# Products with values moved from the middle of a pass's transposes to its head (cross-attention and a mixture of experts, one core)

## The chip, the cores and the metric

One core of a Trainium2 chip runs the whole kernel. The metric is the device time in microseconds (us). Before the change it is 366.25 us, the median of three runs (363.2 to 366.45 us).

## The reference

Eight samples (B = 8) of 112 rows (S) and width 256 attend, with 16 heads of width 16, to a context of 375 rows per sample; then comes a mixture of 32 experts. The attention is what the change touches:

```python
qh = _split_heads(layernorm(x)); kh = vh = _split_heads(ctx)
scores  = einsum('bhqd,bhkd->bhqk', qh, kh) + mask
weights = softmax(scores)
att     = einsum('bhqk,bhkd->bhqd', weights, vh)      # heads joined again
x = x + relu(att @ wo_w.T + wo_b)
x = x + experts(layernorm(x))      # gate, 4 of 32 experts, and a shared one
```

The experts' stage reads the attention's result for all samples, and starts when the attention's block has ended.

## The kernel before, in words

The kernel is written for the engines directly: each engine has its own program, in the order in which it issues, and counting semaphores tie them together. There is no scheduler.

**Tiling of the attention.** Four heads (HPQ = 4) form a group; a sample has four groups (QPB = 4), so there are NQ = 32 groups. TensorE runs a loop over passes p = 0 to 33 (L414). In pass p it works on three groups at once:

- `score(p)` (L358): the scores of group p, four products of 32 rows by 112 by 375, one for each head, into four PSUM banks.
- `turn_prob(4(p-1)+j)` for j = 0 to 3 (L335): the shifted scores `z` of group p-1 are transposed, three pieces of 112 by 125 for a head. The heads' shift by their maximum was done meanwhile: VectorE takes the mask and the maximum of every head (L555), then GpSimd lowers heads 0 and 1 (L289), VectorE head 2 (L565) and ScalarE head 3 (L496). Each head's transposes wait for its own one of these.
- `value(p-2)` (L371): the products of group p-2's weights `pT` with the values, twelve products of 125 rows by 32 by 112, into one bank (SUM_BANK) that holds the sample's sums. It waits until the fourth exponential of group p-2 is there (L373) and, for a sample's first group, for `values_ok` and `sums_ok`.

**The ring of two banks.** Everything that TensorE transposes for ScalarE in this stage goes through two PSUM banks in turn (T_BANK, T_BANK + 1). A unit n, a head's transposes for example, may be written only when ScalarE has read unit n-2 (`bank_of`, L304 to L309). ScalarE reads a head with one exponential, `weigh` (L479), from PSUM to `pT`. `ring_units` (L52) lists the units in order: four heads in each pass and then, at the end of most passes, one more unit by `close(p)` (L349): half the keys of the next sample (k0, k1, three transposes, L316), its queries (q, two transposes, L324) or the attention of an earlier sample (ctxT, two transposes, L332). Passes 3, 28, 29, 30 and 32 have no closing unit.

**Other work in a pass.** In each fourth pass from 8 on, `project` (L397) multiplies with the output weights, after the scores; in passes 6, 10, 14 and so on `turn_sums` (L387) transposes a sample's sums. ScalarE copies these sums out in passes 5, 9 and so on, after the pass's second exponential (`copy_sums`, L475), when all four groups of values have arrived.

**Around it.** Sync issues the loads of context and mask two samples ahead, and behind the masks the loads of the experts' weights (L240 to L250). The last loads of this stage are waited for in the next stage only.

The order inside a pass that the change is about is that of TensorE's loop:

```python
for j in range(HPQ):
    if 0 <= p - 1 < NQ:
        turn_prob(HPQ * (p - 1) + j)
    if j == 1 and p >= 2:
        value(p - 2)
close(p)
```

Of the kernel before, what the change touches and what calls it, by code (L numbers as in the profile page):

```python
# [22 lines left out]
def xattn_moe_kernel(nc, x, ctx, mask, wo_w, wo_b, gw, gb, w1, b1, w3, b3, w2, b2,  # L23
# [61 lines left out]
    with ExitStack() as st:  # L85
# [81 lines left out]
        def attention(block, sba):  # L167
# [129 lines left out]
            def _(pe):  # L297
                def warm(n, bank=SUM_BANK):

                    for _ in range(n):  # L300
                        nc.tensor.matmul(ps[:, bank, :].rearrange("p (r c) -> p r c", c=P), ident[:],  # L301
                                         ident[:].unsqueeze(1).to_broadcast([P, BANK // P, P]), start=True, stop=True)
# [32 lines left out]
                def turn_prob(n):  # L335
                    bank = bank_of(("prob", n))
                    p, j = n // HPQ, n % HPQ
                    if j in POOL_HEADS:
                        pe.wait_ge(by_pool, len(POOL_HEADS) * p + POOL_HEADS.index(j) + 1)
                    elif j in DVE_HEADS:  # L340
                        pe.wait_ge(by_dve, len(DVE_HEADS) * p + DVE_HEADS.index(j) + 1)
                    else:
                        pe.wait_ge(by_act, len(ACT_HEADS) * p + ACT_HEADS.index(j) + 1)
                    for c in range(KT):
                        ins = nc.tensor.transpose(bank[0:KP, c * S:(c + 1) * S], z[:, n % RING, c * KP:(c + 1) * KP],  # L345
                                                  ident[0:S, 0:S])
                    ins.then_inc(ring_full, 1)

                def close(p):  # L349
                    for kind, b in closing(p):  # L350
                        if kind == "q":
                            turn_queries(b)
                        elif kind == "ctxT":
                            turn_att(b)
                        else:
                            turn_keys(b, int(kind[1]))

                def score(p):  # L358
                    b, g = p // QPB, p % QPB
                    if g == 0:  # L360
                        pe.wait_ge(ring_read, max(UNIT["q", b], UNIT["k0", b]) + 1)
                    if g == 2:
                        pe.wait_ge(ring_read, UNIT["k1", b] + 1)
                    if p:
                        pe.wait_ge(masked, HPQ * p)
                    for j in range(HPQ):
                        rows = slice(32 * j, 32 * j + 32)
                        nc.tensor.matmul(ps[0:S, S_BANK + j, 0:SK], qT[rows, b % 2, g // 2, g % 2, :],  # L368
                                         kT[rows, b % 2, g // 2, :], start=True, stop=True).then_inc(scores, 1)

                def value(p):  # L371
                    b, g = p // QPB, p % QPB
                    pe.wait_ge(ring_read, UNIT["prob", HPQ * p + HPQ - 1] + 1)  # L373
                    if g == 0:
                        pe.wait_ge(values_ok, b + 1)
                        if b:
                            pe.wait_ge(sums_ok, b)
                    for c in range(KT):
                        for j in range(HPQ):
                            h = 8 * (g // 2) + 2 * j + g % 2  # L380
                            ins = nc.tensor.matmul(ps[32 * j:32 * j + VC, SUM_BANK, g * S:(g + 1) * S],  # L381
                                                   vaug[:, b % 2, c, h, :],
                                                   pT[:, (HPQ * p + j) % RING, c * S:(c + 1) * S],
                                                   start=(c == 0), stop=(c == KT - 1))
                    ins.then_inc(valued, 1)

                def turn_sums(b):  # L387
                    pe.wait_ge(sums_ok, b + 1)
                    if b:
                        pe.wait_ge(prj_ok, b)  # L390
                    else:
                        pe.wait_ge(wo_copied, 1)
                    for g in range(QPB):
                        ins = nc.tensor.transpose(ps[0:S, AUX_BANK, g * P:(g + 1) * P], sums[:, g * S:(g + 1) * S], ident[:])
                    ins.then_inc(turned, 1)

                def project(b):  # L397

                    pe.wait_ge(ring_read, UNIT["ctxT", b] + 1)
                    pe.wait_ge(att_ok, 2 * b + 2)  # L400
                    for k in range(DK):
                        ins = nc.tensor.matmul(ps[0:S, AUX_BANK, 0:D], attT[:, k, :], woT[:, k, :],
                                               start=(k == 0), stop=(k == DK - 1))
                    ins.then_inc(projected, 1)
# [7 lines left out]
                turn_keys(0, 1)  # L412
                warm(1)
                for p in range(NQ + 2):  # L414
                    if p < NQ:
                        score(p)
                    if p < 2:
                        warm(2)
                    if p == 0:
                        pe.wait_ge(bias_in, 16 * 4)  # L420
                        nc.tensor.transpose(ps[:, AUX_BANK, 0:NE], b1r[:], ident[0:NE, 0:NE])
                        nc.tensor.transpose(ps[:, AUX_BANK, P:P + NE], b3r[:], ident[0:NE, 0:NE]).then_inc(bias_T, 1)
                    if p == 1:
                        pe.wait_ge(bias_copied, 2)
                        pe.wait_ge(wo_in, 16)
                        for t in range(DK):
                            for k in range(DK):
                                ins = nc.tensor.transpose(ps[:, AUX_BANK, (k * DK + t) * P:(k * DK + t + 1) * P],
                                                          wo_raw[:, t, k * P:(k + 1) * P], ident[:])
                        ins.then_inc(bias_T, 1)  # L430
                    if p % QPB == 0 and p >= 2 * QPB:
                        project(p // QPB - 2)
                    if p % QPB == 2 and p > QPB:
                        turn_sums(p // QPB - 1)
                    for j in range(HPQ):
                        if 0 <= p - 1 < NQ:
                            turn_prob(HPQ * (p - 1) + j)
                        if j == 1 and p >= 2:
                            value(p - 2)
                    close(p)  # L440

                pe.wait_ge(masked, HPQ * NQ)
# [712 lines left out]
```

## Time and profile before

| | before |
|---|---|
| median of 3 runs (us) | 366.25 (363.2 to 366.45) |
| profiled execution: its own time / its span (us) | 361.01 / 359.2 |
| TensorE matmul busy, share of the span | 290.2 us, 81% |
| VectorE busy | 222.8 us, 62% |
| GpSimd busy | 181.7 us, 51% |
| ScalarE busy | 150.9 us, 42% |
| mean granted TensorE clock | 0.914 |

All times in the rows further down are microseconds from the start of the span of this one profiled execution, whose own time is 5.24 us below the median of the three runs. The passes 0 to 33 of the attention take from about 13 us to about 150 us; the experts' stage follows from 160 us. A matmul's row is its own duration, and matmuls overlap, so the distance between the starts of two rows tells more than their durations. One product or transpose in float32 shows as one or two rows of the trace, so that "x6" at L345 is the transposes of two heads, "x24" at L381 one `value`, and "x8" at L368 one `score`.

### The profile page before, as it was taken

What the parts mean: (1) busy time and instruction counts of PE and PEld (TensorE: products, weight loads), DVE (VectorE), ACT (ScalarE), POOL (GpSimd) and SP (SyncE); (2) the same over time, 40 slices, a digit from 0 to 9 for tenths busy, and PEclk for the clock granted to TensorE, in tenths of its full rate; (3) what the DMA queues carried; (4) which work ended last, traced back from release to release, by engine and by line L of the source; (5) the groups of instructions that cost most, each with busy time, mean ns of one, the idle gap of its engine ahead of it and who ended that gap; (6) DMA issues with size and microseconds to landing.
All of it is one profiled execution on the core that took longest, in us unless ns stands there. A gap on an engine that the chain in (4) does not pass through costs nothing.

```text
span 359.2 us, 7134 instructions
## 1 busy us (share of the span) xinstructions
PE 290.2 (81%) x2301; PEld 202.9 (56%) x2301; DVE 222.8 (62%) x708; ACT 150.9 (42%) x403; POOL 181.7 (51%) x188
## 2 busy tenths in 40 slices
PE   8999999999999999899898022199999999999000
PEld 3466666666666667656474011077778777776000
DVE  1678877767777778276969200065666666656097
ACT  1267666666566666515110000044545545544000
POOL 7266757565657566110027777307556555556200
PEclk9999999999999999999999555589999999999655
DMA  6795888959794900009502333385555455542495
GB/s 150 206 78 149 261 240 244 265 172 292 218 326 138 308 5 2 2 13 295 162 0 79 109 110 114 116 101 161 162 167 157 148 167 158 155 154 76 159 242 168
DMA packets 54013, 55.92 MB, mean 156 GB/s; under 512 B 18925, under 2 KB 45562, under 8 KB 53466
## 3 DMA queue, kind: packets, MB, share of 16 engines
q1 hardware_dynamic: 49610, 43.94, 45.6%
q0 software_dynamic: 4368, 11.52, 9.8%
q8 instruction: 21, 0.34, 0.4%
q14 instruction: 14, 0.11, 0.1%
HBM read 35.03 MB, written 20.41 MB: 154 GB/s over the span
## 4 chain that ended last, share of the span: by engine, by line
PE 29%; DVE 9%; POOL 9%; issue 4%; DMA 3%; ACT 0%; POOLq 0%; DVEq 0%; SPq 0%
PE ps L878 14%; POOL expert_rows L794 9%; PE ps L893 7%; DVE x L1119 4%; PE ps L870 3%; PE ps L887 2%; DMA b<-expert_out 1%; PE ps L816 1%; DMA expert_rows<-normed,slots 1%; DMA expert_out<-hs,to 1%; DMA xg<-expert_rows 1%; POOL expert_out L799 1%; PE ps L846 1%; PE ps L808 0%; PE ps L841 0%
## 5 line engine op out<-in xcount | busy, mean ns | idle before, releaser
L289 POOL TENSOR_SCALAR z<-z,zmax 112x375 f32<-112x375 f32 x64 | 78.7, 1241 | 52.7 <-DVE zmax L555 52.7
L799 POOL DMA_INDIRECT expert_out<-hs,to x59 | 56.6, 959 | 50.3 <-DVE hs L1088 35.2
L555 DVE CUSTOM_DVE_ANT_0 z<-ps,mask_sb 112x375 f32<-112x375 f32 x128 | 62.5, 546 | 28.8 <-PE ps L368 28.8
L483 ACT ACTIVATE pT<-ps 125x336 f32<-125x336 f32 x128 | 50.7, 448 | 38.1 <-PE ps L345 37.7
L878 PE MATMUL ps<-w,xgT 128*128 x236 | 64.1, 396 | 0.0
L345 PE MATMUL ps<-ident,z 112*125 112x112 f32 x384 | 56.6, 283 | 0.2 <-ACT pT L483 0.2
L345 PEld LDWEIGHTS ps<-ident,z 112*125 112x125 f32 x384 | 47.3, 188 | 15.4 <-ACT pT L483 7.3
L1106 DVE TENSOR_TENSOR hb<-ps,b 128x256 f32<-128x256 f32 x59 | 25.1, 425 | 49.1 <-PE ps L878 49.1
L794 POOL DMA_INDIRECT expert_rows<-normed,slots x32 | 32.4, 1014 | 35.1 <-DVE normed L1059 25.7
L878 PEld LDWEIGHTS ps<-w,xgT 128*128 128x128 f32 x236 | 43.5, 196 | 10.0 <-issue 1.8
L870 PE MATMUL ps<-ident,xg 128*128 128x128 f32 x118 | 24.0, 287 | 30.2 <-DMA xg<-expert_rows 30.2
L935 ACT COPY xgT<-ps 128x256 f32<-128x256 f32 x59 | 22.0, 373 | 46.4 <-PE ps L870 46.4
L893 PE MATMUL ps<-w2s,hs 128*128 x118 | 36.0, 387 | 0.0
L942 ACT COPY hs<-ps 128x128 f32<-128x128 f32 x59 | 15.7, 266 | 47.8 <-PE ps L887 47.8
L870 PEld LDWEIGHTS ps<-ident,xg 128*128 128x128 f32 x118 | 14.8, 146 | 33.2 <-DMA xg<-expert_rows 25.9
L1112 DVE TENSOR_TENSOR hh<-hb,sg 128x128 f32<-128x128 f32 x59 | 17.3, 293 | 19.5 <-ACT sg L947 17.0
L368 PE MATMUL ps<-kT,qT 32*112 32x375 f32 x256 | 28.8, 519 | 0.0
L381 PE MATMUL ps<-pT,vaug 125*32 125x112 f32 x768 | 25.0, 263 | 0.6 <-ACT pT L483 0.6
L1088 DVE COPY hs<-ps 128x256 f32<-128x256 f32 x59 | 24.5, 415 | 1.1 <-PE ps L893 0.6
L301 PE MATMUL ps<-ident 128*128 128x512 f32 x44 | 23.6, 669 | 1.6 <-POOL ident L256 1.6
L565 DVE TENSOR_SCALAR z<-z,zmax 112x375 f32<-112x375 f32 x32 | 23.7, 741 | 0.0
L1119 DVE SCALAR_TENSOR_TENSOR x<-b,gate,x 112x256 f32<-112x256 f32 x32 | 14.9, 484 | 8.9 <-DMA b<-expert_out 8.1
(159 smaller groups left out, 348.8 us busy)
## 6 DMA issues: line engine op xcount, KB each, us to landing
xg<-expert_rows SPq DMA_DIRECT2D x59, 128.0 KB, 2.3
expert_rows<-zero SPq DMA_DIRECT2D x14, 512.0 KB, 10.0
w2s<-in_L_ffn_w SPq DMA_DIRECT2D x2, 2048.0 KB, 9.6
b<-in_L_ffn_b SPq DMA_DIRECT2D x2, 2048.0 KB, 14.1
b<-expert_out SPq DMA_DIRECT2D x8, 448.0 KB, 9.3
ctx_sb<-in_ctx SPq DMA_DIRECT2D x8, 375.0 KB
mask_sb<-in_mask_Bx1xSxS_ff SPq DMA_DIRECT2D x8, 164.1 KB, 2.4
expert_out<-hs,to POOLq DMA_INDIRECT x59, 2.8
```

The source lines that it names most:

```text
L289: pool.tensor_scalar(z[:, n % RING, :], z[:, n % RING, :], zmax[:, n % RING:n % RING + 1], None, ALU.subtract).then_inc(by_pool, 1)
L345: ins = nc.tensor.transpose(bank[0:KP, c * S:(c + 1) * S], z[:, n % RING, c * KP:(c + 1) * KP], ident[0:S, 0:S])
L368: nc.tensor.matmul(ps[0:S, S_BANK + j, 0:SK], qT[rows, b % 2, g // 2, g % 2, :], kT[rows, b % 2, g // 2, :], start=True, stop=True).then_i ...
L483: nc.scalar.activation(pT[:, n % RING, :], ps[0:KP, T_BANK + at % 2, 0:KT * S], ACT.Exp).then_inc(ring_read, 1)
L555: nc.vector.tensor_tensor_reduce(out=z[:, n % RING, :], in0=ps[0:S, S_BANK + j, 0:SK], in1=mask_sb[:, b % 2, :], scale=-1.0 if j in ACT_HE ...
L794: pool.indirect_dma_start(xs, bass.IndirectOffsetOnAxis(ap=slots[:, b, r:r + 1], axis=0), normed[:, b, :], None).then_inc(scattered[r], 16)
L799: pool.indirect_dma_start(ys, bass.IndirectOffsetOnAxis(ap=to[:, j:j + 1], axis=0), y_sb[:, j % 4, :], None).then_inc(y_sent[j % 4], 16)
L870: ins = nc.tensor.transpose(ps[:, T_BANKS[j % 2], k * P:(k + 1) * P], xg[:, j % 4, k * P:(k + 1) * P], ident[:])
L878: ins = nc.tensor.matmul(ps[:, U_BANKS[j % 2], 0:2 * INTER], xgT[:, j % 4, k, :], w13[:, k, bass.ds(owner_of(words, j), 1), :].rearrange(" ...
L893: nc.tensor.matmul(ps[:, Y_BANKS[j % 2], 0:D], hT[:, j % 4, :], w2s[:, bass.ds(owner_of(words, j), 1), :].rearrange("p o c -> p (o c)"), s ...
L1106: TT(hb[:, j % 2, :], ps[:, U_BANKS[j % 2], 0:2 * INTER], b13[:, bass.ds(owner_of(words, j), 1), :].rearrange("p o c -> p (o c)"), ALU.add ...
L1119: ins = nc.vector.scalar_tensor_tensor(x2[:, b, :], rows[:, TOPK * b + r, :], gate[:, b, r:r + 1], x2[:, b, :], ALU.mult, ALU.add)
```

## The change

`value(p - 2)` is issued at the head of pass p, ahead of `score(p)`, where before it stood between the transposes of the pass's second and third head. Nothing else is changed: the same instructions with the same waits and the same semaphores, in another order on TensorE alone. No DMA is moved, and no other engine's program.

```diff
@@ -412,6 +412,8 @@
                 turn_keys(0, 1)
                 warm(1)
                 for p in range(NQ + 2):
+                    if p >= 2:
+                        value(p - 2)
                     if p < NQ:
                         score(p)
                     if p < 2:
@@ -435,8 +437,6 @@
                     for j in range(HPQ):
                         if 0 <= p - 1 < NQ:
                             turn_prob(HPQ * (p - 1) + j)
-                        if j == 1 and p >= 2:
-                            value(p - 2)
                     close(p)
 
                 pe.wait_ge(masked, HPQ * NQ)
```

## Rows read from the trace of the kernel before

**Rows 1.** The page: busy tenths of 40 equal slices, and the granted clock
```profile
PE   8999999999999999899898022199999999999000
PEclk9999999999999999999999555589999999999655
```

**Rows 2.** Windows by stage: busy us (instructions) of each engine, PEclk, DMA share, GB/s
```profile
60.00:100.00 40.00, 38.08 (x469) 27.01 (x470) 29.79 (x102) 25.53 (x61) 25.23 (x22) 1.00 0.79 232
140.00:152.00 12.00, 10.80 (x142) 7.52 (x134) 5.79 (x20) 7.26 (x16) 4.11 (x4) 1.00 0.01 1
198.00:236.00 38.00, 9.24 (x27) 6.42 (x28) 3.73 (x11) 2.87 (x10) 23.33 (x25) 0.51 0.43 110
```

**Rows 3.** Timeline of TensorE, pass 17 and the start of 18: start, us, what, idle before
```profile
84.61 0.90 PE L368 MATMUL ps<-kT,qT 32*112 32x375 f32 x8
85.44 0.91 PE L345 MATMUL ps<-ident,z 112*125 112x112 f32 x6
86.28 0.78 PE L381 MATMUL ps<-pT,vaug 125*32 125x112 f32 x24
86.99 0.91 PE L345 MATMUL ps<-ident,z 112*125 112x112 f32 x6
88.11 0.54 PE L316 MATMUL ps<-ident,ctx_sb 125*128 125x125 f32 x3 [0.21 <-ACT pT L483]
88.58 0.90 PE L368 MATMUL ps<-kT,qT 32*112 32x375 f32 x8
```

**Rows 4.** Timeline of ScalarE in the same pass
```profile
86.05 0.79 ACT L483 ACTIVATE pT<-ps 125x336 f32<-125x336 f32 x2 [0.36 <-PE ps L345]
87.12 0.53 ACT L477 COPY sums<-ps 128x448 f32<-128x448 f32 x1 [0.28 <-PE ps L381]
87.60 0.79 ACT L483 ACTIVATE pT<-ps 125x336 f32<-125x336 f32 x2
```

**Rows 5.** The line of the exponential: durations min/median/max in ns, 20 to 150 us
```profile
L483 ACT ACTIVATE pT<-ps x128: 444/451/452, 20.9 to 149.0; 125x336 f32<-125x336 f32 x128
```

**Rows 6.** Timeline of pass 1, which has no value products: TensorE (weight loads PEld) and ScalarE
```profile
19.96 0.60 PE L428 MATMUL ps<-ident,wo_raw 128*128 128x128 f32 x4
20.29 0.73 PEld L345 LDWEIGHTS ps<-ident,z 112*125 112x125 f32 x6
20.40 0.81 PE L345 MATMUL ps<-ident,z 112*125 112x112 f32 x6
20.92 0.79 ACT L483 ACTIVATE pT<-ps 125x336 f32<-125x336 f32 x2 [1.22 <-PE ps L345]
21.42 0.92 PE L345 MATMUL ps<-ident,z 112*125 112x112 f32 x6 [0.21 <-ACT pT L483]
22.54 0.54 PE L316 MATMUL ps<-ident,ctx_sb 125*128 125x125 f32 x3 [0.20 <-ACT pT L483]
```

**Rows 7.** Timeline of TensorE where a pass (29) has no closing unit
```profile
136.81 0.91 PE L345 MATMUL ps<-ident,z 112*125 112x112 f32 x6
137.65 0.58 PE L368 MATMUL ps<-kT,qT 32*112 32x375 f32 x4
```

**Rows 8.** Timeline of TensorE, end of pass 31, passes 32 and 33
```profile
144.75 0.41 PE L332 MATMUL ps<-ident,att 112*128 112x112 f32 x2 [0.21 <-ACT pT L483]
145.60 1.12 PE L402 MATMUL ps<-woT,attT 128*112 128x256 f32 x4 [0.43 <-ACT attT L472]
147.29 0.78 PE L381 MATMUL ps<-pT,vaug 125*32 125x112 f32 x24
148.00 0.91 PE L345 MATMUL ps<-ident,z 112*125 112x112 f32 x6
149.46 0.78 PE L381 MATMUL ps<-pT,vaug 125*32 125x112 f32 x24 [0.55 <-ACT pT L483]
```

**Rows 9.** Timeline of TensorE where the closing unit is a pair of transposes (passes 14, 15)
```profile
75.61 0.41 PE L324 MATMUL ps<-ident,normed 112*128 112x112 f32 x2 [0.21 <-ACT pT L483]
75.95 0.90 PE L368 MATMUL ps<-kT,qT 32*112 32x375 f32 x8
```

**Rows 10.** Timeline of GpSimd in pass 17
```profile
86.29 2.44 POOL L289 TENSOR_SCALAR z<-z,zmax 112x375 f32<-112x375 f32 x2 [2.38 <-DVE zmax L555]
```

**Rows 11.** Chain of waits, start and us: the same four matmuls at either clock
```profile
233.11 1.78 PE ps L878 x4
236.09 0.86 PE ps L878 x4
```

## The prediction

> **What bounds the kernel now.** I read the slices first. TensorE is busy in eight or nine tenths from the start to about 160 us, and in this whole stretch its granted clock stays at the full level (2.4 GHz) [rows 1]. The windows say who could bind there: from 60 to 100 us TensorE has 38.1 of 40 us, VectorE 29.8, ScalarE 25.5, GpSimd 25.2 [rows 2]. A busy TensorE may still be waiting, so the timeline of a pass comes next. Pass 17 runs from 84.61 to 88.58, that is 3.97 us: scores 0.83, two heads' transposes 0.84, values 0.71, two heads' transposes and what follows 1.12, keys 0.47 [rows 3]. The reader is to see that no part waits except the closing unit (0.21 us by the profile, "<-ACT pT"). So the stage goes at the pace at which TensorE issues plus one wait a pass for a bank of the ring, and what is added between two starts on TensorE is added to the end: the experts' stage begins behind it and nothing overlaps the two.
>
> **How long a bank of the ring is held.** Call T0 to T3 the four heads' transposes, V the values, C the closing unit, S the scores. T2 starts at 86.99 [rows 3] and ScalarE's exponential on it at 87.60 [rows 4], 0.61 us later; it takes 0.45 us [rows 5], so the bank is read at 88.05, and C, which needs this bank, starts at 88.11 [rows 3]: 1.12 us from the start of a head's transposes to the next use of its bank. The transposes of two heads take 0.84 us (85.44 to 86.28), so whoever follows two heads directly waits 1.12 - 0.84 = 0.28 us. The profile counts 0.21 us of it, because the last matmul's modelled end is later than its issue.
>
> **What the change does to T2.** Today V stands between T1 and T2. T0 starts at 85.44, its exponential at 86.05 [rows 4], its bank is free at about 86.56; T1 is done at 86.28 and V covers until 86.99. With V gone T2 is ready at 86.28 and waits until 86.56: 0.28 us. T2 starts 1.12 after T0, T3 needs no wait (T1's exponential follows 0.35 us behind T0's, and T3 0.42 behind T2), and C comes 1.12 after T2 as before. So T0 to C is 2.24 us plus V elsewhere, against 2.67 with V inside: 2.24 + 0.71 - 2.67 = +0.28 us a pass.
>
> The trace of before has one pass in just the new form: pass 1, where there is no V yet. The profile shows both waits there, 0.21 us at 21.42 and 0.20 us at 22.54 [rows 6]. From the first weight load of T0 (20.29) to C (22.54) it is 2.25 us. This is the row on which I rest the term.
>
> **What V costs at its new place.** Before a C of three transposes V would start at T2 + 1.12 + 0.47 = T2 + 1.59; it needs T3's exponential, which pass 33 shows: T2 at 148.00, V at 149.46, that is T2 + 1.46 [rows 8]. Behind a C of two transposes C takes 0.34 us (75.61 to 75.95) [rows 9], so V is at T2 + 1.46 too, just on time. So V does not wait where a pass closes with a unit. S comes behind V then; that pair no row shows. The nearest rows are V then T2 (0.71 us from start to start) and C then S (0.47 for three transposes) [rows 3]. Unbroken transposes come every 0.11 us (four at L428, 19.96 to 20.40) [rows 6], so six are 0.66 and the 0.84 of rows 3 hold 0.18 for two changes of form, about 0.09 each. I take V then S at 0.71, as V then T2; the ends are 0.62 (no price for the change of form) and 0.80 (twice). Over 30 passes that is -2.7 or +2.7 us.
>
> Where a pass has no closing unit nothing covers T3's exponential. Today S follows 0.84 us after T2 (136.81 to 137.65) [rows 7]; V can start only at T2 + 1.46, so +0.62 us for each of the passes 3, 28, 29 and 30 (the profile's own figure for this wait in pass 33 is 0.55 [rows 8]).
>
> ScalarE's copy of the sums stands between the second and third exponential in seven passes. Today it runs in V's shadow (87.12, the next exponential at 87.60) [rows 4]. Now T0's exponential is at 86.05, T1's at 86.40, the copy at 86.75, and T2's exponential can begin at 87.23 instead of 86.56 + 0.61 = 87.17: +0.06, seven times, +0.4 us.
>
> The end gives something back. C of pass 31 starts at 144.75, and the projection waits for ScalarE's copy until 145.60, 0.85 us [rows 8]. V fits in there: the projection then starts at 144.75 + 0.34 + 0.71 = 145.80, and V is gone from between T1 and T2. That is 0.71 - 0.20 = 0.51 saved and 0.28 lost at T2: -0.23 us.
>
> **What is hidden.** S comes later in no chain that binds: GpSimd, the last to deliver, starts 1.68 us after S and ends at 88.73 [rows 10], and its second head is wanted by T1 of the next pass, at 88.58 + 0.83 + 0.42 = 89.83 at the earliest. That is 1.1 us of slack, and the distance from S to T0 and T1 of the next pass grows by the longer pass. Without that cover each us of lateness would be a us a pass. T2 and T3 stand 0.43 us earlier against it, but VectorE and ScalarE deliver them. No queue of Sync or GpSimd is passed by V; the loads behind the masks come up to 9 us later, and DMA is idle at 1% from 140 to 152 us [rows 2].
>
> **Sum.** 30 passes (2 to 31) x 0.28 = 8.4; 4 x 0.62 = 2.5; copies 0.4; pass 32 -0.2. Together +11.0 us. Against the profiled execution: 361.0 + 11.0 = 372.0 us. The runs' median is 5.2 us above that execution; on it the sum gives **377.3 us**, 3.0% more. Lower bound of the terms: 30 x 0.20 + 4 x 0.55 - 0.2 - 2.7 = +5.3; upper: 11.0 + 2.7 = +13.7.
>
> **Rivals.**
> 1. *Not slower: the change of form is saved and the wait doesn't come.* V no longer breaks the transposes, so a pass has three changes of form instead of four: 30 x 0.09 = 2.7 us less, and 0.5 less in pass 32: -3.2, 363.0 us. It decides if T0's exponential is read 0.84 us after T0's start rather than 1.12. For it speaks the 0.09 worked out above; against it the wait in pass 1 [rows 6], which swallows the saving, as it would here. Chance 0.06. The Trainium skill (TensorEngine Tiling (Array Packing), Key Properties) says that changing the tiling mode drains TensorE; taken alone, that rule gives this rival's time. The trace agrees that such a change costs something, and shows that the wait stands ahead of it.
> 2. *The wait only moves.* T2 waits 0.28 and C no longer does. Only the four bare passes and the copies are left, +2.7 us: 369 us. It needs T2's exponential to be sooner than T0's; pass 1 shows both waits in one pass [rows 6]. Chance 0.06.
> 3. *V waits behind the closing unit too.* The margin is 0.13 us behind keys and nothing behind a pair. If T3's exponential comes 0.2 us later than I have it in 26 passes, 5.2 us more: 382.5 us. Against it: pass 33 shows the distance directly. Chance 0.10.
> 4. *The granted clock falls.* With two short waits in a pass TensorE might be granted the lower level (1.2 GHz), at which four matmuls take 1.78 us instead of 0.86 [rows 11]. A pass at that level would take some 3.5 us more; ten of them 35 us, 412 us in all. Against it: pass 1 has both waits, and the clock falls only at 198 us, where TensorE is busy for 9 of 38 us [rows 1, 2]. Chance 0.02. The Trainium skill (TensorE: Matmul & The Clock Gate, A second HAM failure mode: psum-queue depth-cycling) says that short idles between groups of matmuls that cycle through PSUM banks can make the clock swing; no row here shows it, although one such wait a pass is there already.
>
> **Numbers.** The forecast has 0.76. About 1% (3.7 us) is what a measurement of this kernel can tell from no change. Slower by more holds the forecast and rivals 3 and 4: 0.88. Rival 2 (+0.7%) and half of rival 1 (-0.9%) are within 1%: 0.09; the other half faster: 0.03. Range: the lower bound gives 371.6, less 1.6 for runs that spread over 3.3 us: 370; the top takes in rival 3: 383. Outside are rivals 1, 2 and 4, 0.14, and a little of the forecast's own scatter.
>
> **What would show it.** Pass 17 of after: 4.3 us from S to S; in every pass a wait of about 0.2 us at L345 in front of the third head as well as at the closing unit; V starting 0.34 or 0.47 us after C, without a wait; L381 waiting about 0.5 us in passes 4, 29, 30, 31 and 33; S 0.71 us behind V; the attention's last projection some 11 us later, and the experts' stage of the same length. I am wrong if L345 shows no such wait, if V waits in most passes, or if the experts' stage changes its length.

## Result and profile after

The changed kernel takes 376.02 us (median of four runs, 374.64 to 377.63) against 365.0 us before in the same comparison: ratio 1.0306, 95% interval 1.0227 to 1.0385. It is slower, by 11 us. The forecast was 377.3 us.

I measure the attention from the start of the scores of pass 1 to the start of the values of pass 33, and call that the stage. Before it goes from 17.31 to 149.46, 132.15 us; after, from 17.06 to 159.98, 142.92 us. That is +10.77 us. The slices of the changed kernel, which answer to [rows 1]:

```profile
PE   8998898999999998899989121296999999999100
PEclk9999999999999999999999755579899999999655
```

The reader is to see that the granted clock stays full through the whole attention, so the time was not lost by a lower clock. TensorE's timeline of pass 17 shows where it was lost, the counterpart of [rows 3] (start, us, what, idle before):

```profile
89.23 0.78 PE L381 MATMUL ps<-pT,vaug 125*32 125x112 f32 x24
89.94 0.90 PE L368 MATMUL ps<-kT,qT 32*112 32x375 f32 x8
90.78 0.91 PE L345 MATMUL ps<-ident,z 112*125 112x112 f32 x6
91.89 0.92 PE L345 MATMUL ps<-ident,z 112*125 112x112 f32 x6 [0.21 <-ACT pT L483]
93.02 0.54 PE L316 MATMUL ps<-ident,ctx_sb 125*128 125x125 f32 x3 [0.20 <-ACT pT L483]
93.48 0.78 PE L381 MATMUL ps<-pT,vaug 125*32 125x112 f32 x24
94.20 0.90 PE L368 MATMUL ps<-kT,qT 32*112 32x375 f32 x8
```

The pass takes 4.26 us (89.94 to 94.20) instead of 3.97. There are two waits for a bank now, 1.12 us from the first head (90.78) to the third (91.89), and again from there to the keys (93.02). Keys to values is 0.46 us without a wait, values to scores 0.72. The list of TensorE's waits from 23 to 162 us (us in total, times, longest) begins with these entries:

```profile
PE ps L345 <- ACT pT L483: 6.6, 31, 0.2
PE ps L381 <- ACT pT L483: 2.7, 5, 0.5
PE ps L316 <- ACT pT L483: 2.4, 12, 0.2
```

L345 and L381 are what is new: before, L345 has no wait from 23 us on and L381 one, of 0.55 us in pass 33 [rows 8], while L316 had its twelve waits already (2.6 us in total). L345, the heads' transposes, waits once in each of passes 2 to 32; L381, the values, five times: in passes 4, 29, 30, 31 and 33. Nothing waits for VectorE or GpSimd. The first of the four at the end of the stage comes behind pass 28, which has no closing unit and answers to [rows 7]; the values at 143.08 are the head of pass 29:

```profile
140.60 0.81 PE L345 MATMUL ps<-ident,z 112*125 112x112 f32 x6
141.62 0.92 PE L345 MATMUL ps<-ident,z 112*125 112x112 f32 x6 [0.21 <-ACT pT L483]
143.08 0.78 PE L381 MATMUL ps<-pT,vaug 125*32 125x112 f32 x24 [0.54 <-ACT pT L483]
143.79 0.90 PE L368 MATMUL ps<-kT,qT 32*112 32x375 f32 x8
```

From the third head to the values it is 1.46 us; before, the scores followed after 0.84. And the end, the counterpart of [rows 8]:

```profile
155.50 0.41 PE L332 MATMUL ps<-ident,att 112*128 112x112 f32 x2 [0.20 <-ACT pT L483]
155.84 0.78 PE L381 MATMUL ps<-pT,vaug 125*32 125x112 f32 x24
156.55 1.12 PE L402 MATMUL ps<-woT,attT 128*112 128x256 f32 x4
159.98 0.78 PE L381 MATMUL ps<-pT,vaug 125*32 125x112 f32 x24 [0.54 <-ACT pT L483]
```

The values stand where TensorE waited for ScalarE's copy; from the closing unit to the last values it is 4.48 us (155.50 to 159.98) instead of 4.71 (144.75 to 149.46).

### The profile page after: what moved, and what is told of

Its sections match the earlier page's. It is cut to its first block, busy times and chain, and to the rows that moved or that the text cites. A ratio compares the mean times of both kernels' runs of the same rounds, so it can differ in the third digit from the quotient of the medians.

```text
span 375.6 us, 7134 instructions
## 1 busy us (share of the span) xinstructions
PE 295.6 (79%) x2301; PEld 205.4 (55%) x2301; DVE 223.0 (59%) x708; ACT 149.9 (40%) x403; POOL 182.1 (48%) x188
## 4 chain that ended last, share of the span: by engine, by line
PE 25%; issue 18%; DVE 5%; DMA 2%; SPq 2%; another core or an unknown queue 1%; ACT 1%; POOL 1%; POOLq 0%; DVEq 0%
PE ps L878 13%; PE ps L893 6%; DVE x L1119 4%; PE ps L870 3%; PE ps L887 2%; SPq L750 1%; DMA b<-expert_out 1%; DMA expert_out<-hs,to 1%; POOL expert_out L799 1%; DMA xg<-expert_rows 0%; POOLq L1127 0%; ACT sg L947 0%; ACT xgT L935 0%; SPq L755 0%
## 5 line engine op out<-in xcount | busy, mean ns | idle before, releaser
L878 PE MATMUL ps<-w,xgT 128*128 x236 | 66.0, 405 | 0.0
L345 PE MATMUL ps<-ident,z 112*125 112x112 f32 x384 | 57.0, 284 | 6.8 <-ACT pT L483 6.8
L345 PEld LDWEIGHTS ps<-ident,z 112*125 112x125 f32 x384 | 47.7, 187 | 22.2 <-ACT pT L483 12.5
L878 PEld LDWEIGHTS ps<-w,xgT 128*128 128x128 f32 x236 | 44.7, 201 | 10.6 <-issue 2.2
L381 PE MATMUL ps<-pT,vaug 125*32 125x112 f32 x768 | 25.0, 263 | 2.7 <-ACT pT L483 2.7
L301 PE MATMUL ps<-ident 128*128 128x512 f32 x44 | 23.3, 660 | 1.6 <-POOL ident L256 1.6
L381 PEld LDWEIGHTS ps<-pT,vaug 125*32 125x32 f32 x768 | 17.3, 109 | 7.7 <-ACT pT L483 5.7
```

What stands on the lines that cost most here:

```text
L878: ins = nc.tensor.matmul(ps[:, U_BANKS[j % 2], 0:2 * INTER], xgT[:, j % 4, k, :], w13[:, k, bass.ds(owner_of(words, j), 1), :].rearrange(" ...
```

## Experiments

Of each I give the stage as defined above, from one profile. In four of the twelve profiles (the changed kernel's third, values behind the third head, and the last two kernels below) the granted clock fell to about half for 3.4 us from 18 us on, and pass 1 is some 1.7 us longer; there I compare from the scores of pass 2, where the kernel before has 126.45 us. These are the four in which TensorE had waited longest in pass 0 for the load of `b3r`, one of the experts' biases: 1.46 to 1.89 us, against 0.52 to 1.33 us in the eight others.

**The changed kernel and the one before again.** Both unchanged.

> The changed kernel again, for the experts' stage, which was 5.6 us longer in its profile than in that of before. If that belongs to the change, it is there again; if it was ScalarE's 3.2 us pause and the lower clock behind it in that one execution, this profile has the attention at 142.9 us again and an experts' stage within 2 us of that of before.

> The kernel before once more, for a second profile. Stage from the scores of pass 1 to the values of pass 33: 132.2 us. The pause of ScalarE near the tenth block of the experts (about 3 us, seen in both profiles of the changed kernel and not in the one of before): if it belongs to the change it is absent here; if it comes with the chip or the moment, it can be here too.

> The changed kernel a third time beside it: stage 142.9 us. If the pause belongs to the change it is here and not in the kernel before; if not, the two profiles agree on it or it falls either way.

Stage of the changed kernel: 142.90 us in the first repetition (its median 376.94 us), and 144.62 in the second with the low clock in pass 1 (136.51 from the scores of pass 2, the same to 0.01 us as in the first profile). Before: 132.15 again. The first repetition, in four runs, was at 1.0336 (1.0273 to 1.04) of the one before. The attention's length is thus repeatable to 0.02 us, and the +10.8 us are the change's.

The experts' stage is another matter. From its first transposes to the end of the span the profile of before has 199.2 us and the second of the same kernel 204.1; the changed kernel has 205.1, 202.1 and 205.2. What differs is a pause of ScalarE. ScalarE's timeline in the changed kernel's first profile, behind an instruction that ended at 257.26:

```profile
260.44 0.27 ACT L942 COPY hs<-ps 128x128 f32<-128x128 f32 x1 [3.17 <-remote]
```

and in the second profile of the kernel before:

```profile
249.47 0.37 ACT L935 COPY xgT<-ps 128x256 f32<-128x256 f32 x1 [1.17 <-remote]
```

The pause comes with either kernel, and "remote" says that the profile knows no source for it. In both of these the clock fell for 3.4 us behind it (262.3 and 250.9 us). Over all twelve profiles, whose experts' stages have the same instructions, the seven with such a pause have an experts' stage of 202.1 to 205.2 us and the five without it 199.2 to 200.4. By these it goes with the moment of the execution and not with the kernel: the first four of the experiments' kernels that were measured together (the repetition, the two other places and the values behind the scores) all have it, the four of the shorter exponential, the fillers and the split all lack it. So it is no part of the change. The profile of before on which the prediction was worked out was one without it, and the pause's 4.9 us (204.1 against 199.2) would account for most of the 5.2 us by which it lay below its runs' median.

**Values at the other places among the transposes.** In the two kernels that follow, ScalarE's copy of the sums is moved too, so that it does not stand and wait for the values in the middle of the heads.

```diff
-                        if j == 1 and p >= 2:
+                        if j == 2 and p >= 2:
                             value(p - 2)
...
-                        if j == 1 and p % QPB == 1 and p > QPB:
+                        if j == 3 and p % QPB == 1 and p > QPB:
                             copy_sums(p // QPB - 1)
```

> Values between the third and fourth head's transposes (and ScalarE's copy of the sums moved behind the fourth exponential, so that it doesn't wait for them in the middle). Measured by the stage from the scores of pass 1 to the values of pass 33: 132.2 us before, 142.9 us after. Theory (a bank is held 1.12 us from the start of a head's transposes, so each neighbouring pair of gaps between the five ring units needs 0.28 us of other work): the third head waits 0.28 us, but the values then cover the closing unit's wait, so 26 passes cost nothing; the four bare passes and pass 32 cost 0.28 each: 133.6 us, about +1.4. Rival (any place but the one between second and third head costs a wait more, as in the changed kernel): +9 or more.

Measured: stage 137.29 us. Two windows from 17 to 26 us, of this kernel and of the one before, show that part of it is the clock in pass 1 (busy us of TensorE, its weight loads, VectorE, ScalarE and GpSimd, then the granted clock, 0.81 against 1.00, the DMA's share and its GB/s):

```profile
17.00:26.00 9.00, 8.41 (x44) 4.60 (x44) 5.07 (x18) 4.51 (x9) 4.64 (x5) 0.81 1.01 95
```
```profile
17.00:26.00 9.00, 8.59 (x77) 5.54 (x77) 6.40 (x25) 5.62 (x11) 6.04 (x6) 1.00 1.05 95
```

From the scores of pass 2 it is 129.94 us, +3.5 on before, where the theory had +1.4 and the rival +9. Over the whole it ran at 1.010 of the kernel before (1.002 to 1.0181). Pass 9:

```profile
53.77 0.90 PE L368 MATMUL ps<-kT,qT 32*112 32x375 f32 x8
54.60 0.91 PE L345 MATMUL ps<-ident,z 112*125 112x112 f32 x6
55.72 0.58 PE L345 MATMUL ps<-ident,z 112*125 112x112 f32 x3 [0.21 <-ACT pT L483]
56.23 0.78 PE L381 MATMUL ps<-pT,vaug 125*32 125x112 f32 x24
56.94 0.58 PE L345 MATMUL ps<-ident,z 112*125 112x112 f32 x3
57.36 0.48 PE L316 MATMUL ps<-ident,ctx_sb 125*128 125x125 f32 x3
57.77 0.90 PE L368 MATMUL ps<-kT,qT 32*112 32x375 f32 x8
```

The wait at the third head is there, the one at the keys is gone, and the pass takes 4.00 us against 3.97. The mechanism holds, the rival falls. The 2.1 us that I had too little are in small places: a bare pass costs 0.47 more than before (3.68 against 3.21 us), not 0.28, because one head's transposes alone take 0.51 us from the wait to the values and not 0.42 (the change of form at their end); the closing passes cost 0.03 us each; pass 30 costs 0.2 us more, between the scores and the sums' transposes, which now wait for the moved copy; and passes 31 to 33 together cost 0.63 us where I had 0.28.

```diff
-                        if j == 1 and p >= 2:
+                        if j == 3 and p >= 2:
                             value(p - 2)
```

> Values behind the fourth head's transposes, ahead of the closing unit (copy of the sums behind the fourth exponential). Theory: the third head waits 0.28 us, the closing unit no more; four bare passes +0.28 each; in pass 32 the values cover the last wait, -0.3: stage 132.9 us, +0.8 on before. Rival: values at an end of the transposes cost both waits whichever end it is: 140 us or more.

Measured: the stage costs 1.2 us more than before (its one run took 366.7 us). Its end has to be read with care, for the values of passes 32 and 33 stand in one row, as nothing lies between them:

```profile
149.98 1.39 PE L381 MATMUL ps<-pT,vaug 125*32 125x112 f32 x48
151.31 1.98 PE L301 MATMUL ps<-ident 128*128 128x512 f32 x4
```

The second half of the first row, which is pass 33's, starts 0.61 us behind the first half, at about 150.6, so the stage is 133.3 us. The product behind it (L301) says the same: it comes 134.03 us behind the scores of pass 1 (17.28), where before it came 132.87 us behind them (150.18 and 17.31). The theory had +0.8, the rival +8 or more. Pass 13 has one wait, now at the third head, and none at the keys:

```profile
68.98 0.91 PE L345 MATMUL ps<-ident,z 112*125 112x112 f32 x6
70.10 0.92 PE L345 MATMUL ps<-ident,z 112*125 112x112 f32 x6 [0.21 <-ACT pT L483]
70.95 0.78 PE L381 MATMUL ps<-pT,vaug 125*32 125x112 f32 x24
71.66 0.54 PE L316 MATMUL ps<-ident,ctx_sb 125*128 125x125 f32 x3
```

So taking the values from between the second and third head is not what costs; putting them where they cover no wait is.

**Values behind the scores.** The changed kernel with the two exchanged:

```diff
-                    if p >= 2:
-                        value(p - 2)
                     if p < NQ:
                         score(p)
+                    if p >= 2:
+                        value(p - 2)
```

> Values behind the scores instead of ahead of them, otherwise the changed kernel. Theory: both bank waits remain (30 x 0.28 = 8.4 us), but the four waits of 0.62 us for the fourth exponential in the bare passes are covered by the scores: stage 142.9 - 2.5 = 140.4 us, the whole kernel about 2.5 us below the changed one, still 2% slower than before. Rival (holding back the scores is what costs, through VectorE and GpSimd): the stage would fall back to about 132 us.

Measured: stage 140.46 us; the whole at 1.0258 (1.0193 to 1.0323) of the kernel before, where the changed kernel, measured beside it, had 1.0336. Pass 29, bare, and the next scores:

```profile
143.36 0.91 PE L345 MATMUL ps<-ident,z 112*125 112x112 f32 x6
144.48 0.92 PE L345 MATMUL ps<-ident,z 112*125 112x112 f32 x6 [0.21 <-ACT pT L483]
145.33 0.90 PE L368 MATMUL ps<-kT,qT 32*112 32x375 f32 x8
```

The wait for the third head is there, that for the fourth exponential is covered by the scores. The stage gives up 2.46 us, which is 4 x 0.62. The scores now go first and nothing comes back beyond that: holding them back had cost nothing.

**A shorter exponential**, in the kernel before and in the changed one. ScalarE reads 112 of the 336 columns of a head, so that the softmax is left out for two thirds of the keys and the kernel's result is not the reference's; only the order of the work and its times are read from it. The diff is the same for both (the waits for the fill are left out here):

```diff
-                    nc.scalar.activation(pT[:, n % RING, :], ps[0:KP, T_BANK + at % 2, 0:KT * S],
+                    nc.scalar.activation(pT[:, n % RING, 0:S], ps[0:KP, T_BANK + at % 2, 0:S],
...
+                pool.memset(pT[:], 1.0).then_inc(values_zero, 1)
```

> The kernel before, with each exponential over the first 112 of its 336 columns; the other weights are left at 1 (a fill at the start), so the softmax is left out for two thirds of the keys. From the durations at 448, 336 and 224 columns (0.53, 0.45, 0.35 us) an exponential over 112 takes about 0.26 us, so a bank is held 0.93 us instead of 1.12 and the one wait of a pass falls from 0.28 to 0.09: stage (scores of pass 1 to values of pass 33) 132.2 - 5 = 127 us. If the wait had another source than ScalarE's read, the stage would stay at 132 us.

> The same shortened exponential (two thirds of each softmax left out) in the changed kernel. Both waits of a pass fall to 0.09 us and the bare passes' by 0.19: 142.9 - 56 x 0.19 - 6 x 0.19 = about 131 us, so that what the change costs falls from 10.8 to about 4 us. If the change costs through the order alone (the scores held back, changes of form), the two kernels stay 10.8 us apart.

Measured: an exponential takes 0.26 us instead of 0.45, and the stage 126.72 us before the change and 130.86 with it. TensorE in the kernel before (pass 11), and TensorE and ScalarE in the changed one (pass 13); the lines' numbers are one higher here:

```profile
59.75 0.91 PE L346 MATMUL ps<-ident,z 112*125 112x112 f32 x6
60.68 0.41 PE L333 MATMUL ps<-ident,att 112*128 112x112 f32 x2
```
```profile
68.58 1.84 PE L346 MATMUL ps<-ident,z 112*125 112x112 f32 x12
69.19 0.59 ACT L484 ACTIVATE pT<-ps 125x112 f32<-125x112 f32 x2 [1.07 <-PE ps L346]
70.44 0.54 PE L317 MATMUL ps<-ident,ctx_sb 125*128 125x125 f32 x3
```

A bank is held 0.93 us (59.75 to 60.68), and from the first head to the keys the changed kernel needs 1.86 us (68.58 to 70.44) instead of 2.24. What the change costs falls from 10.8 to 4.1 us, and the one run of each says the same (356.43 and 360.44 us), with nothing of the order touched: what shrank is the time that ScalarE reads a bank. That shows the cause: the order costs only as much as the exponential outlasts the work beside it.

**Other cover for the waits.** If each bank's hold must be covered, the one wait of the kernel before can be covered too. In passes 8, 12 and so on the projection, in passes 6, 10 and so on the sums' transposes, go from behind the scores to ahead of the closing unit:

```diff
-                    if p % QPB == 0 and p >= 2 * QPB:
-                        project(p // QPB - 2)
-                    if p % QPB == 2 and p > QPB:
-                        turn_sums(p // QPB - 1)
                     for j in range(HPQ):
...
                             value(p - 2)
+                    if p % QPB == 0 and p >= 2 * QPB:
+                        project(p // QPB - 2)
+                    if p % QPB == 2 and p > QPB:
+                        turn_sums(p // QPB - 1)
                     close(p)
```

> The kernel before, with the projection and the transposes of the sums moved from behind the scores to behind the fourth head's transposes, ahead of the closing unit. Theory: in 11 passes that close with a unit this work covers the wait of 0.28 us: stage 132.2 - 3.1 = 129.1 us. Rival (VectorE, which divides and adds the residual behind it, comes too late for the next scores): the same 132 us or more.

Measured: stage 128.97 us, but with the low clock in pass 1; from the scores of pass 2 it is 121.58, so -4.9 us instead of -3.1. Its one run took 358.15 us. Pass 12 shows where the rest comes from:

```profile
65.80 0.91 PE L345 MATMUL ps<-ident,z 112*125 112x112 f32 x6
66.54 1.03 PE L402 MATMUL ps<-woT,attT 128*112 128x256 f32 x4
67.41 0.49 PE L316 MATMUL ps<-ident,ctx_sb 125*128 125x125 f32 x3
67.82 0.90 PE L368 MATMUL ps<-kT,qT 32*112 32x375 f32 x8
```

Heads, projection and keys follow at 0.74, 0.87 and 0.41 us, where they took 0.84, 0.95 and 0.47 when each stood next to products of another form; the pass's first two heads, now directly behind the scores, take 0.10 more. With the wait of 0.28 a pass with the projection is 0.42 us shorter (five times) and one with the sums' transposes 0.38 (six times), 4.4 us, and passes 28 to 33 are 0.5 shorter together. Behind pass 29 the rival is seen once: that pass is 0.38 us longer than before, and the scores of pass 30 wait for VectorE's maximum.

```profile
135.34 0.90 PE L368 MATMUL ps<-kT,qT 32*112 32x375 f32 x8 [0.31 <-DVE zmax L555]
```

**The version that beats both.** To this the values are split in the other closing passes, and ScalarE's copy of the sums moves behind the fourth exponential (the edit is shown in part):

```diff
+                        late = closing(p) and not (p % QPB == 0 and p >= 2 * QPB) and not (p % QPB == 2 and p > QPB)
                         if j == 1 and p >= 2:
-                            value(p - 2)
+                            value(p - 2, range(KT - 1) if late else range(KT))
+                        if j == 3 and p >= 2 and late:
+                            value(p - 2, range(KT - 1, KT))
```

> As the one with the projection and sums as cover, and in the closing passes without them two thirds of the values stay between the second and third head and the last third stands ahead of the closing unit (the copy of the sums behind the fourth exponential). Theory: no bank wait is left; a split costs a second change of form each way, so from the first head's transposes to the closing unit 0.84 + 0.52 + 0.84 + 0.32 = 2.52 us instead of 2.67: 15 x 0.15 + 11 x 0.28 = 5.3 us less, stage 126.8 us, 1.4% faster than before. Rival (the pieces cost more than the wait that they cover): stage 129 us or more, no difference that can be measured.

Measured: 354.33 us (median of seven runs, 354.13 to 357.02) against 362.18 for the kernel before beside it, ratio 0.9785 (0.9746 to 0.9825): faster than before, by 1.8 to 2.5%. Stage 126.76 us, again with the low clock in pass 1; from the scores of pass 2 it is 119.41, -7.0 us, of which 4.9 are the fillers' and the rest 0.14 or 0.15 us in each pass with split values. Pass 17 takes 3.83 us and has no wait:

```profile
83.00 0.90 PE L368 MATMUL ps<-kT,qT 32*112 32x375 f32 x8
83.83 0.91 PE L345 MATMUL ps<-ident,z 112*125 112x112 f32 x6
84.67 0.59 PE L381 MATMUL ps<-pT,vaug 125*32 125x112 f32 x16
85.19 0.91 PE L345 MATMUL ps<-ident,z 112*125 112x112 f32 x6
86.03 0.40 PE L381 MATMUL ps<-pT,vaug 125*32 125x112 f32 x8
86.36 0.54 PE L316 MATMUL ps<-ident,ctx_sb 125*128 125x125 f32 x3
86.83 0.90 PE L368 MATMUL ps<-kT,qT 32*112 32x375 f32 x8
```

From the first head to the keys it is 2.53 us (83.83 to 86.36), as expected at 2.52.

## Why the prediction was right

- **The number.** 377.3 us forecast, 376.02 measured. The growth forecast was 11.0 us, on a kernel before of 366.25 us; in the comparison that kernel took 365.0, and that is the 1.3 us between them.
- **What bounds the stage.** TensorE's issue and its waits for banks set it. The stage grew by 10.77 us, the medians by 11.0 us. That these agree with the sum to the last tenth is partly luck: the interval of the ratio allows 8 to 14 us, and the sum has a term that did not come (the copies, below).
- **The wait at the third head.** 0.28 us in each of 30 passes, taken from pass 1 [rows 6]: the waits list has it 31 times, with the one of pass 32, and pass 17 grew by 0.29 us. The shortened exponential shows that ScalarE's read sets it.
- **The pair that no row showed.** Values to scores is 0.72 us, as taken (0.71), with ends of 0.62 and 0.80.
- **Bare passes.** 1.46 us from third head to values in the changed kernel, +0.62, and 2.46 us for the four when the scores cover them again.
- **The copy of the sums.** This term, +0.4 us, was wrong and is zero. In pass 17, which has the copy, the closing unit comes 2.24 us behind the first head, as it does in pass 19, which has none (99.54 to 101.78). I had the copy and the exponential behind it 0.35 and 0.48 us apart; ScalarE took 0.33 and 0.44 (start, us, what):

```profile
91.39 0.79 ACT L483 ACTIVATE pT<-ps 125x336 f32<-125x336 f32 x2 [1.07 <-PE ps L345]
92.07 0.54 ACT L477 COPY sums<-ps 128x448 f32<-128x448 f32 x1
92.51 0.80 ACT L483 ACTIVATE pT<-ps 125x336 f32<-125x336 f32 x2
```

  The third exponential starts at 92.51, 0.62 us behind its transposes (91.89), just when its input is there.
- **Pass 32.** -0.23 us forecast, and 4.48 against 4.71 measured.
- **The sum.** Without the copies' term it is 8.4 + 2.5 - 0.2 = 10.7 us; measured 10.77.
- **What was hidden.** Nothing of VectorE's or GpSimd's stands in TensorE's waits, and with the scores back in front the stage changed only by the bare passes.
- **The experts' stage** of the same length: the two first profiles differ (205.1 against 199.2 us), which the prediction had named as a sign of being wrong; but the kernel before itself has 199.2 and 204.1, with ScalarE's pause in the second alone. Where neither order had the pause, with the shorter exponential, the stage is 199.9 us before the change and 199.95 with it. So the forecast holds for the change.

Rival 1, that the change of form is saved without a wait, and rival 2, that the wait only moves, fell with the two waits of pass 17. Moving the wait is what values behind the third and behind the fourth head do (+3.5 and +1.2 us), not this change. Rival 3 would have shown as values waiting behind a closing unit; there is none. Rival 4 did not come: in the first two profiles of the changed kernel the clock is full throughout the attention although there are two waits in each pass, and in the third it fell once, in pass 1, behind the wait for `b3r` and before the first moved values. Its price was set a little low: there 3.4 us at the lower level cost 1.7 us, half of them, by which a pass of 4 us would cost some 4 us more, not 3.5.

TensorE drains at a change of tiling mode, says the Trainium skill (TensorEngine Tiling (Array Packing), Key Properties). The trace agrees that the change costs time, and does not show the drain itself: beside products of another form the projection takes 0.95 us and not 0.87, and two heads' transposes 0.84 and not 0.74. In the changed kernel the saved change of form was swallowed by the wait, as forecast; it came back only where cover took the wait's place.

## What to carry to other kernels

In the orders tried here what follows placed every wait for a bank. With a ring of two buffers, write down for each unit how long its buffer is held (here 1.12 us from the first transpose to the release) and add up what the producer issues between a unit and the one after the next; each sum that is smaller is a wait, and a filler covers the two sums on either side of its place. A filler put next to another one, where its cover is not needed, is wasted, as here the values beside the scores at the head of the pass. Before such work is moved, look for a stretch in the trace in which it is missing: pass 1 showed the new order with both waits.

## Of the hardware, not expected

- A change of the products' form (the rows and columns of the array that they take) costs 0.06 to 0.11 us at each end in the rows read here, so that grouping the full-array work (heads, projection or sums, keys) gained 0.10 to 0.14 us in each of eleven passes beyond the wait.
- ScalarE paused 1.2 to 3.4 us near the tenth block of the experts in seven of twelve profiles, in one of two of the kernel before, and the granted clock sometimes fell for 3.4 us behind it. Where it comes from stays open.
- In four profiles the granted clock fell for 3.4 us near 18 us and cost 1.7 us in pass 1; the first and the third profile of the changed kernel differ in the attention by just that. It fell behind the four longest waits for `b3r`, and behind none of the eight shorter ones. No run varied that wait, so that it is the cause is not shown.
